# Four triangle layers on one core: the multiplied planes laid out row by row instead of plane by plane

## What is computed

```python
xn = layernorm(group_norm(x))
left  = (xn @ Wl + bl) * sigmoid(xn @ Wlg + blg) * mask
right = (xn @ Wr + br) * sigmoid(xn @ Wrg + brg) * mask
t = einsum('bikd,bjkd->bijd', left, right)      # layers 0, 1
t = einsum('bkjd,bkid->bijd', left, right)      # layers 2, 3
x = x + (layernorm(t) * sigmoid(xn @ Wog)) @ Wout   # in layers 1 and 3 the gate comes last
```

## Time and profile before

| | before |
|---|---|
| runs | 1708.82, 1697.83, 1710.12 us; median 1708.82 |
| the profiled execution | 1708.89 us, its span 1706.9 us |
| TensorE, matmul records | 1431.6 us busy, 84% of the span |
| TensorE, weight loads | 908.1 us, 53% |
| VectorE | 967.4 us, 57% |
| ScalarE | 1083.2 us, 63% |
| granted TensorE clock, mean | 0.917 |

### The profile page before, as it was taken

The page is one execution under the profiler, slowest core; times in us unless marked ns, Lnnn a source line. Parts: engine busy times, 40 slices in busy tenths (PEclk is TensorE's granted clock), DMA queues, the critical chain, the costliest instruction groups (busy, mean ns, idle before and its releaser), DMA issues. The chain is left out here.

```text
span 1706.9 us, 43804 instructions
## 1 busy us (share of the span) xinstructions
PE 1431.6 (84%) x12950; PEld 908.1 (53%) x12950; DVE 967.4 (57%) x2784; ACT 1083.2 (63%) x2381; POOL 384.8 (23%) x345
## 2 busy tenths in 40 slices
PE   0899997899888887989941888889898777798998
PEld 0444443677644444757731555557566433366665
DVE  6477772455568887217740666642166688820455
ACT  0788873666478886229941888852377688822564
POOL 0233320232233332004420333310033300000334
PEclk9999998955589999999975999999899999999999
DMA  7011115676523222457876232224599844346799
GB/s 246 29 50 47 46 52 135 198 213 204 180 80 98 95 92 72 140 157 233 262 189 164 88 98 92 97 85 149 137 271 293 246 139 138 130 121 176 231 306 284
DMA packets 213029, 258.75 MB, mean 152 GB/s; under 512 B 29408, under 2 KB 202848, under 8 KB 212960
## 3 DMA queue, kind: packets, MB, share of 16 engines
q1 hardware_dynamic: 212960, 257.86, 50.2%
HBM read 149.26 MB, written 108.53 MB: 151 GB/s over the span
## 5 line engine op out<-in xcount | busy, mean ns | idle before, releaser
L967 DVE SCALAR_TENSOR_TENSOR lr<-ps,mask,act_out 128x128 f32 (+5 forms) x1152 | 282.6, 311 | 81.7 <-ACT act_out L712 78.6
L1117 POOL TENSOR_TENSOR rstd<-ve,half_col 128x6 f32<-128x6 f32 x144 | 190.4, 1323 | 464.2 <-DVE ve L940 464.2
L489 PE MATMUL ps<-w_parts,val 64*128 64x256 bf16 (+1 forms) x2112 | 214.3, 304 | 38.6 <-DVE lr L967 34.1
L594 PEld LDWEIGHTS ps<-k,sq 128*128 128x128 f32 x1152 | 186.7, 222 | 63.8 <-issue 16.6
L712 ACT ACTIVATE act_out<-ps 128x384 f32<-128x384 f32 x384 | 190.4, 497 | 20.1 <-PE ps L496 17.6
L1148 POOL TENSOR_TENSOR new_ring<-val,res_ring 128x384 f32<-128x384 f32 x96 | 95.9, 1000 | 455.7 <-DVE val L1052 401.7
L489 PEld LDWEIGHTS ps<-w_parts,val 64*128 64x128 bf16 (+1 forms) x2112 | 90.5, 111 | 190.3 <-DVE lr L967 153.1
L1033 DVE TENSOR_TENSOR xn<-ps,cen 128x384 f32<-128x384 f32 x192 | 107.1, 558 | 124.6 <-PE ps L602 113.3
L1137 POOL TENSOR_TENSOR val<-act_out,gate_ring 128x384 f32<-128x384 f32 x96 | 96.0, 1000 | 341.8 <-ACT act_out L794 290.3
L760 ACT ACTIVATE in_ring<-ps 128x768 f32<-128x768 f32 (+1 forms) x64 | 51.9, 811 | 183.5 <-PE ps L545 161.0
L594 PE MATMUL ps<-k,sq 128*128 128x2 f32 x1152 | 161.2, 256 | 0.0
(11 more groups left out here) (96 smaller groups left out, 2451.7 us busy)
## 6 DMA issues: line engine op xcount, KB each, us to landing
gate_scratch<-gate_ring SPq DMA_DIRECT2D x192, 192.0 KB, 2.3
gate_ring<-gate_scratch SPq DMA_DIRECT2D x96, 384.0 KB, 4.2
in_ring<-x_scratch SPq DMA_DIRECT2D x144, 192.0 KB, 2.4
in_ring<-t_scratch SPq DMA_DIRECT2D x144, 192.0 KB, 4.5
res_ring<-x_scratch SPq DMA_DIRECT2D x72, 384.0 KB, 5.2
x_scratch<-new_ring SPq DMA_DIRECT2D x48, 384.0 KB, 2.9
t_scratch<-in_ring SPq DMA_DIRECT2D x48, 384.0 KB, 2.7
lr<-x SPq DMA_DIRECT2D x6, 1536.0 KB, 16.0
```

What stands on the lines that cost most here:

```text
L489: nc.tensor.matmul(banks[h][:, :, 0:P], moving(x, s)[half(h), N * r:N * r + P], proj_weights(w, h)[:, 0:2 * P], start=start, stop=stop, sk ...
L594: mm = nc.tensor.matmul(ps[:, 6 + s % 2, 2 * j:2 * j + 2], sq[:, s % 2, P * j:P * j + P], k_sel, start=True, stop=True)
L967: ins = nc.vector.scalar_tensor_tensor(out5[:, h, lo // 2:hi // 2, :, m], ps[:, 4 + 2 * r + h, lo:hi].rearrange("p (a e) -> p a e", e=2), ...
L1117: nc.gpsimd.tensor_tensor(rstd[:, s % 2, :], ve[:, s % 2, :], half_col[:, :], ALU.pow)\
```

## The change

One line of `lr_view` changes. The flat buffer is now cut into 192 picture rows of 192 elements, and the planes lie side by side within a row. Nothing else in the code changes: the same instructions, in the same order, on the same engines.

```diff
@@ -170,7 +170,7 @@
         def lr_view(l):
 
             flat = lr[:, :].bitcast(BF16)[:, 0:COLS * N] if l == 0 else lr[:, :]
-            return flat.rearrange("p (a r e) -> p a e r", r=N, e=2)
+            return flat.rearrange("p (r a e) -> p a e r", r=N, e=2)
```

## The result

The changed kernel takes 1939.17 us (median of 4 runs, 1906.53 to 1949.28), the kernel before 1703.32 us (median of 4, 1673.36 to 1710.12). The ratio is 1.138, with an interval of 1.092 to 1.184: slower, as forecast, but above the range's end of 1925 us. The profiled execution took 1906.53 us with a span of 1904.6 us.

The account below looks back on a forecast made before the run. TensorE was taken to set the length of B1 in layers 1 to 3. The sum: 1708.9 + 141 (f32 moving operand) + 3 (layer 0) + 2 (left for B2) = 1855 us, range 1697 to 1925 us.

Parts of the forecast that it names:

- What bounds the kernel: B1 of layers 1 to 3: TensorE sets the length, so every ns its matmuls get goes into the kernel's time.
- The sign: Whole kernel: slower by more than 1%, about 17 us, with a chance of 0.68.
- VectorE's gain of 0: VectorE's writes of lr in phase A: pairs cost nothing, so dense rows gain 0; L967 stays at 346 and 276 ns.
- The weight loads, costed at nothing: TensorE's weight loads in B1: a 128-column load rises from 193 to 306 ns, still below 320 ns, adding nothing.
- their cover is the slower matmul: B1: weight loads overlap the matmul before, whose doubled record of 320 ns hides loads of 306 ns.
- second rival: B1: only weight loads slow down, the moving operand is free; +38 us, 1747 us; chance 0.06.
- The f32 moving operand, +141 us: B1 of layers 1 to 3: streaming takes twice as long, two groups 13.7 us in place of 7.82; +141 us.
- Layer 0, +3 us: B1 of layer 0: doubled bf16 streaming gives 2.0 us a group, under the 2.34 the stores allow; +3 us.
- The bound of 320 ns a record and +20 us: B1 of layer 0: if bf16 falls to 320 ns a read, two groups take 7.2 us; +20 us.
- each of the 7.82 us doubles: B1 of layers 1 to 3, upper bound: all of the two groups' time doubles; +188 us.
- The first rival: TensorE's reads in B1: the step is free, time 1709 us within 1%; chance 0.26.
- The third: B1's narrow records: worse than double, pairs no longer gained, +184 us on top of 1855, 2040 us; chance 0.06.
- The fourth: Layer 0's B2: keeps its high clock, 34 us come off, 1675 us; chance 0.05.

Follow-up runs that it names:

- Weights alone: Kernel before, but in phase B1 only the weights read with a step of 192 elements, layout unchanged: 1744.92 us, beside 1710.74 for the kernel before.
- the moving operand alone: Kernel before, but in phase B1 only the moving operand read with a step of 192 elements, layout unchanged: 1901.92 us, beside 1710.74.
- The fillers: Kernel before with a filler matmul of 384 f32 columns ahead of each output matmul in layer 0's B2: 1676.0 us, beside 1700.28.

## Why the prediction was wrong, point by point

What bounds the kernel was right: B1 of layers 1 to 3 is TensorE's, the copies wait for it, and the change went straight into the time. The sign and the mechanism, a step of single elements at half pace, held for the moving operand. VectorE's gain of 0 held (345 and 276 ns).

Three terms of the sum were too small, by about 100 us together. The weights had been given nothing, and layer 0 came out above its bound.

- **The weight loads, costed at nothing.** This is the step that failed: "their cover is the slower matmul". Weights alone cost 39 us in layers 1 to 3, my own second rival's price, and they cost about as much on top of the slower moving operand (71.1 us in layer 3, of which the moving operand alone is 55.5, so 16 us where the weights alone cost 13). I had made a rival of what was an addend. A load's duration below the matmul's, 314 ns for 338, does not prove that it is hidden.
- **The f32 moving operand, +141 us.** Alone it costs 54.0 + 55.3 + 55.5 = 165 us. Wide main records were near the forecast (338 ns for 320); the narrow kinds, read two at a time, took 3.28 us where 2.86 was forecast. A part may be what a step of 768 bytes costs more than one of 752 or 784, 11 to 13 us a layer when both operands have it; with the moving operand alone it was not measured, and nothing in the trace of before could show it.
- **Layer 0, +3 us.** It is +35. I doubled a bf16 record to 160 ns; the cost goes by the 16-byte line, so that it became 374 ns. The bound of 320 ns a record and +20 us was in the text, and was the better guess. B1 of layer 0 is 33 us longer, 27 of them with the moving operand alone; the fall of the clock to 0.52 in that stage cost its slow reads nothing, as the equal 1.66 us at both levels show.

Together 211 + 35 = 246 us stand where 146 were forecast. The upper end, "each of the 7.82 us doubles", was no bound: 16.73 is 2.14 times 7.82. The moving operand alone makes 1.89 times (14.77 us), and the weights alone add 1.7 us; the bound had only one of the two in it.

The first rival (free) is excluded. The third does not hold: narrow records still run as pairs, one every 231 ns and not every 320. Pairs on the same partitions have the longer latency (719 ns for 515), but take no more time than the others, 3.69 and 3.72 us for 16. The fourth, layer 0's B2 at the high clock, does happen: in the profiled execution after. The kernel before has runs of 1663 to 1673 us that fit it, though none of them was profiled (1662.74, 1662.87 and 1669.4 us had mean clocks of 0.956, 0.951 and 0.95). I had priced it at 34 us and 1675. The fillers bring it about without the change.

## What to carry to other kernels

Lay out what TensorE reads so that successive elements share a 16-byte line: two f32 or four bf16, and where another engine writes across, interleave pairs, so that both have company in the line. When both operands get the bad step and TensorE sets the stage's length, price moving operand and weights as two costs and add them, and count in lines, not in elements. A group of rows by shape can still mix layers and types; cut the window to one layer before reading its mean. Where a stage's clock falls by chance, one filler matmul a tile can hold it (24 to 26 us here), and it makes comparisons sharper.

## What the runs showed of the hardware that was not expected

- TensorE reads at nearly full pace up to 8 bytes between f32 elements (B1 62.5 to 65.3 us, 59.9 to 61.2 dense) and at full pace at 4 bytes between bf16 elements (83 ns for 192). From 16 bytes on both cost about 1.8 ns an element (338 ns for 192 columns in f32 and 336 in bf16, with the moving operand alone).
- Reads that are slow by their step go at the same pace at both levels of the clock (1.66 us for four bf16 records at 1.00 and at 0.50); dense ones do not (0.78 and 1.40 us for eight).
- A step of 768 bytes costs some 10% more than a neighbouring one (133.6 us, 122.2 at 752, 120.6 with rows of 784); 256 and 512 bytes are as slow (134.3 and 133.6). Why 64 bytes is the cheapest of the large steps, 115.0 us, is open.
- The granted clock stayed at 0.97 to 0.99 in the f32 stages where reads were slow, but stood at 0.52 in the bf16 stage with as slow reads. What tells the two apart was not tried.
- VectorE pays for writing single elements: (430 - 304)/64 = 1.97 ns an element in f32 and (895 - 679)/64 = 3.4 ns in bf16, for 1.09 in pairs in both.
